# A mixture-of-experts decoder block: tile order of the late experts, and pair loads moved into the expert stage

## What is computed

```python
def _L0_ffn_ref(x, router_w, up_proj, down_proj):     # E = 8, TOP_K = 2, D = 256
    logits = jnp.einsum('nh,eh->ne', xt, router_w)
    probs = jax.nn.softmax(logits, axis=-1)
    scores, expert_idx = jax.lax.top_k(probs, TOP_K)
    scores = scores / jnp.sum(scores, axis=-1, keepdims=True)
    gate = jnp.zeros((N, E)).at[jnp.arange(N)[:, None], expert_idx].add(scores)
    h = jnp.einsum('nh,ehd->end', xt, up_proj)
    hidden = jax.nn.silu(h[..., :D]) * h[..., D:]
    out_e = jnp.einsum('end,edh->enh', hidden, down_proj)
    out = jnp.einsum('ne,enh->nh', gate, out_e)
...
x = _layernorm(x + _L0_ffn_ref(x, ...), axis=-1)
```

## Time and profile before

| | us |
| --- | --- |
| median of 3 runs | 238.61 (238.19 to 240.59) |
| profiled execution, its own time | 238.29 |
| its span, first to last instruction | 236.5 |
| PE busy | 197.6 (84%) |
| DVE busy | 162.2 (69%) |
| POOL busy | 147.9 (63%) |
| ACT busy | 116.0 (49%) |

### The profile page before, as it was taken

One profiled execution on the slowest core, in us unless ns is written; L12 is line 12 of the kernel. 1 busy time (PEld: TensorE's weight loads), 2 busy tenths in 40 slices (PEclk: granted clock), 3 DMA queues, 4 the chain that ended last, 5 costly groups with the idle time before them and its releaser, 6 DMA issues.

```text
span 236.5 us, 4774 instructions
## 1 busy us (share of the span) xinstructions
PE 197.6 (84%) x1351; PEld 175.3 (74%) x1351; DVE 162.2 (69%) x524; ACT 116.0 (49%) x296; POOL 147.9 (63%) x136
## 2 busy tenths in 40 slices
PE   7756989999999989988999999999999999970000
PEld 6646878989988878976788888888888888850000
DVE  3966688988899888674787666656656655640484
ACT  3261324525344337964887455545545544540194
POOL 0446669586596850937576477777777777541770
PEclk9999999999999999979999999999999999997555
DMA  6963356777666301213333133332332334213994
GB/s 233 394 262 136 133 206 178 240 195 241 225 182 187 85 1 62 77 14 99 92 95 109 45 93 104 113 95 75 95 111 75 92 97 107 67 35 120 413 353 181
DMA packets 18073, 33.80 MB, mean 143 GB/s; under 512 B 5662, under 2 KB 8482, under 8 KB 18050
## 3 DMA queue, kind: packets, MB, share of 16 engines
q1 hardware_dynamic: 13586, 21.80, 27.8%
q0 software_dynamic: 3744, 9.35, 13.6%
q10 hardware_dynamic: 720, 2.36, 2.6%
HBM read 25.09 MB, written 9.33 MB: 146 GB/s over the span
## 4 chain that ended last, share of the span: by engine, by line
PE 56%; DVE 12%; POOL 9%; DMA 8%; issue 7%; ACT 6%; POOLq 1%; SPq 0%; DVEq 0%; ACTq 0%
PE p_c L713 11%; PE p_y L520 6%; PE p_v L713 5%; DMA space<-y_dram 4%; POOL keep L1521 4%; POOL y_dram L1544 4%; PE p_v L463 4%; PE p_y L741 3%; PE p_s L505 3%; PE p_s L713 2%; PE p_a L713 2%; PE p_r L713 2%; PE p_c L480 2%; PE p_t L756 2%; PE p_a L536 2%
## 5 line engine op out<-in xcount | busy, mean ns | idle before, releaser
L1544 POOL DMA_INDIRECT y_dram<-keep,scatter_idx x39 | 39.1, 1002 | 20.9 <-issue 10.3
L1521 POOL DMA_INDIRECT keep<-x_dram,gather_idx x39 | 38.4, 984 | 15.5 <-issue 9.5
L713 PE MATMUL p_c<-w_hi,parts 128*128 x104 | 34.6, 414 | 0.0
L1246 DVE TENSOR_TENSOR cs<-p_c,cs 128x256 f32<-128x256 f32 x26 | 11.0, 424 | 22.3 <-ACT cs L1428 22.2
L1489 POOL TENSOR_TENSOR w_lo<-keep,w_hi 128x1536 f32 (+1 forms) x7 | 24.1, 3446 | 0.0
L1416 ACT ACTIVATE parts<-p_y 128x256 fp32r<-128x256 f32 x39 | 14.9, 381 | 18.6 <-PE p_y L741 18.6
L713 PEld LDWEIGHTS p_c<-w_hi,parts 128*128 128x128 f32 x104 | 17.6, 189 | 2.5 <-issue 0.2
L1428 ACT ACTIVATE cs<-p_c 128x256 f32<-128x256 f32 x26 | 10.0, 385 | 18.2 <-PE p_c L713 18.2
L1239 DVE TENSOR_TENSOR parts<-p_y,parts 128x256 fp32r<-128x256 f32 x39 | 16.5, 423 | 2.9 <-ACT parts L1416 2.6
L713 PE MATMUL p_v<-w_hi,parts 128*128 x52 | 17.3, 415 | 0.0
L1250 DVE TENSOR_TENSOR parts<-p_t,parts 128x256 fp32r<-128x256 f32 x39 | 16.2, 414 | 0.6 <-ACT parts L1434 0.6
(11 more groups left out here) (279 smaller groups left out, 531.2 us busy)
## 6 DMA issues: line engine op xcount, KB each, us to landing
keep<-in_weights SPq DMA_DIRECT2D x8, 768.0 KB, 4.6
space<-in_xT SPq DMA_DIRECT2D x8, 256.0 KB, 3.6
keep<-in_x SPq DMA_DIRECT2D x8, 256.0 KB, 3.3
space<-in_ctxT SPq DMA_DIRECT2D x8, 256.0 KB, 3.2
space<-in_ctxt SPq DMA_DIRECT2D x8, 256.0 KB, 3.3
x_dram<-x SPq DMA_DIRECT2D x8, 256.0 KB, 3.6
space<-y_dram SPq DMA_DIRECT2D x4, 512.0 KB, 8.0
space<-y_dram ACTq DMA_DIRECT2D x4, 512.0 KB, 8.3
```

The lines of the kernel that those rows point to most:

```text
L713: last = nc.tensor.matmul(dst, lhs[:, k, :], w[:].rearrange("p e n -> p (e n)")[:, bass.ds(start + col + k * width, width)], start=(n == 0 ...
L1521: nc.gpsimd.indirect_dma_start(xs[k % HELD], None, x2_dram, bass.IndirectOffsetOnAxis(ap=gather_idx[:, k:k + 1], axis=0)).then_inc(xs_ok[k ...
L1544: nc.gpsimd.indirect_dma_start(y_dram, bass.IndirectOffsetOnAxis(ap=scatter_idx[:, k - 2:k - 1], axis=0), xs[s][:, 0:D], None, bounds_chec ...
```

## The change

The late tiles are put in order of the group of pairs that their first row belongs to (sequences 0 to 9, 10 to 13, 14 and 15) and by expert within a group. So all rows of pairs 0 to 4 lie in the first 27 tiles and those of pairs 5 and 6 in the first 35. SP loads pair 0 when 27 tiles have been scattered, pairs 1 to 4 after one more tile each, pairs 5 and 6 after 35, and pair 7 after all 39. POOL adds pairs 0 to 4 in steps 36 to 40 of the pipeline, behind that step's scatter, and pairs 5 and 6 behind the pipeline. The sum stays in the loaded buffer, since the old place of the results still holds tiles. The late routing has more steps (a running sum over 24 counts instead of 8); `LATE_INVERSE` becomes 9, late gathers go out three tiles ahead instead of four, and POOL makes three late rows where DVE made four.

```diff
-LATE_INVERSE = 8
+LATE_INVERSE = 9
+GROUPS = 3
+FIRST_DONE, NEXT_DONE = ((b * T * TOPK + E * (P - 1)) // P for b in (EB, B - 2))
-ACT_LATE, DVE_LATE = (20, 21, 22, 23, 24, 26, 27, 28), (25, 29, 30, 31)
+ACT_LATE, POOL_LATE = (20, 21, 22, 23, 24, 26, 27, 28, 29), (25, 30, 31)
...
-            for s in range(HELD):
-                sp.wait_ge(put_ok[s], 16 * len(range(s, TILES, HELD)))
-            for j in range(0, PAIRS, 2):
+            for j in range(EB // 2):
+                wait_for_tiles(FIRST_DONE + j)
+                load_pair(j)
+            for j in range(EB // 2, PAIRS - 1):
+                wait_for_tiles(NEXT_DONE)
+                load_pair(j)
+            wait_for_tiles(TILES)
+            load_pair(PAIRS - 1)
...
                 if k == 0:
-                    running(1)
-                    note("later", nc.vector.tensor_scalar(later[:, NE:], tile_in[:, NE:], HIDE, None, ALU.add))
-                    running(2)
+                    for n in range(5):
+                        by = 2 ** n
+                        after_op("run")
+                        note("run", nc.vector.tensor_tensor(run[n + 1][:, LEAD:], run[n][:, LEAD:],
+                                                            run[n][:, LEAD - by:LEAD - by + GROUPS * E], ALU.add))
...
+            pair_scales(0, 3)
+            pair_stats(3)
+            pair_stats(4)
+            pair_moments(3)
+            pair_moments(4)
+            pair_stats(5)
+            pair_scales(3, 5)
+            pair_stats(6)
+            pair_moments(5)
+            pair_moments(6)
+            pair_scales(5, 7)
+            second_half(6)
+            dve.wait_ge(y_back[7], 16)
+            nc.vector.tensor_tensor(res[:, 7, :, :], y_all[:, 7, :, 0, :], y_all[:, 7, :, 1, :], ALU.add).then_inc(r3_ok, 1)
+            pair_stats(7)
+            pair_moments(7)
+            pair_scales(7, 8)
+            second_half(7)
...
+            pair_roots(3, 5)
+            act.wait_ge(shift3_ok, 2)
+            pair_rows(3, 2)
+            pair_rows(4, 2)
+            pair_roots(5, 7)
+            act.wait_ge(shift3_ok, 3)
+            pair_rows(5, 2)
+            pair_rows(6, 1)
+            pair_roots(7, 8)
...
-                if k + 4 == ET:
+                if k + 3 == ET:
                     pool.wait_ge(gates_saved, 64)
                     pool.wait_ge(gather_ok, 2)
-                if k + 4 >= ET and has(4):
-                    gather(k + 4)
+                if k + 3 >= ET and has(3):
+                    gather(k + 3)
...
+                if 6 <= k < 6 + len(POOL_LATE):
+                    if k == 6:
+                        pool.wait_ge(row_no_ok, 2)
+                    make_row(POOL_LATE[k - 6])
+                if k >= TILES - 3:
+                    add_pair(k - TILES + 3)
```

More of the change, by code:

```diff
@@ L220, in decoder_block @@
         full = sb("full", [P, E])
-        offset_e = sb("offset_e", [P, E])
+        need_l = sb("need_l", [P, 2, E])
+        before_ceil = sb("before_ceil", [P, E])
+        looks = sb("looks", [P, 5, E])
+        offsets = sb("offsets", [P, 2, E])
+        run = [sb(f"run{n}", [P, LEAD + GROUPS * E]) for n in range(6)]
+        wanted = turns[:].rearrange("p h d -> p (h d)")[:, 0:5 * NL * E].rearrange("p (w n e) -> p w n e", w=5, e=E)
+        found = sb("found", [P, 5, NL])
+        passed = sb("passed", [P, 2, NL])
+        moved = sb("moved", [P, 2, NL])
+        partial = [sb(f"partial{n}", [P, NL]) for n in range(2)]
+        flat = sb("flat", [P, LT])
+        wraps = [sb(f"wraps{n}", [P, LT]) for n in range(3)]
         bounds = turns[:].rearrange("p h d -> p (h d)")[:, 0:2 * NE * E].rearrange("p (w n e) -> p w n e", w=2, e=E)
         ends = sb("ends", [P, 2, NE])
-        off = back[:].rearrange("p q h d -> p (q h d)").bitcast(F16)[:, 0:(len(ACT_EARLY) + len(ACT_LATE)) * P].rearrange(
+        off = back[:].rearrange("p q h d -> p (q h d)").bitcast(F16)[:, 0:2 * len(ACT_EARLY) * P].rearrange(
             "p (n r) -> p n r", r=P)
@@ L700, in _ @@
             before(place_l[:, 0:LB, :], EB, B, False)
-            for b in range(EB, B):
-                last = above(place_l[:, b - EB + 1:, :], b, False)
+            for b in range(EB, B - 2):
+                above(place_l[:, b - EB + 1:, :], b, False)
+            above(place_l[:, LB - 1:LB, :], B - 2, False)
+            for b in range(B - 2, B):
+                last = above(place_l[:, LB + 1:, :], b, False)
             last.then_inc(place_ok, 1)
@@ L786, in _ @@
                 nc.vector.memset(upto[n][:], 0.0).then_inc(clear_ok, 1)
+            for n in range(6):
+                nc.vector.memset(run[n][:, 0:LEAD], 0.0).then_inc(clear_ok, 1)
             nc.vector.memset(eps[:], EPS).then_inc(eps_ok, 1)
@@ L1162, in _ @@
             dve.wait_ge(rank_ok, 2)
-            note("tiles", nc.vector.tensor_scalar(offset_e[:], need[:], ROUND, -ROUND, ALU.add, ALU.add))
+            note("looks", nc.vector.tensor_scalar(looks[:, 2:4, :], need_l[:], ROUND, -ROUND, ALU.add, ALU.add))
             def late_routing(k):
@@ new lines, in late_routing @@
+                if k == 2:
+                    after_op("delta")
+                    note("wanted", nc.vector.tensor_tensor(wanted, pick[:, NE:, :].unsqueeze(1).to_broadcast([P, 5, NL, E]),
+                                                           looks[:].unsqueeze(2).to_broadcast([P, 5, NL, E]), ALU.mult))
+                    gates(EB, B, 0)
+                if k == 3:
+                    after_op("wanted")
+                    note("found", nc.vector.tensor_reduce(found[:], wanted, AX_X, ALU.add))
+                    gates(EB, B, 1)
@@ L1198, in late_routing @@
                     after_op("tile_from")
-                    note("tile_no", nc.vector.tensor_tensor(tile_no[:], tile_from[:], later[:], ALU.add))
-                if k == 3 or k == 4:
-                    rows = slice(0, TOPK * B // 2) if k == 3 else slice(TOPK * B // 2, TOPK * B)
+                    note("tile_no", nc.vector.scalar_tensor_tensor(tile_no[:, 0:NE], tile_from[:, 0:NE], -HIDE, later[:, 0:NE],
+                                                                   ALU.add, ALU.add))
@@ L1202, in late_routing @@
+                if k == 6 or k == 7:
+                    rows = slice(0, TOPK * B // 2) if k == 6 else slice(TOPK * B // 2, TOPK * B)
                     after_op("tile_no")
@@ L1230, in late_routing, with pair_stats, pair_moments @@
                                             ALU.min, ALU.mult).then_inc(index_ok, 1)
+                if k == LATE_INVERSE + 3:
                     targets(inv_l, late, 1)
[L1232 removed]
+                if k == LATE_INVERSE + 4:
                     targets(inv_l, late, 2)
+                if k == TILES:
+                    pair_stats(0)
+                if k == TILES + 1:
+                    pair_stats(1)
+                    pair_moments(0)
+                    pair_stats(2)
+                    pair_moments(1)
+                    pair_moments(2)
+            def pair_stats(j):
+                dve.wait_ge(r3_ok, j + 1)
+                for q in range(2):
+                    nc.vector.bn_stats(st3[:, j, q, :], res[:, j, q, :]).then_inc(st3_ok, 1)
+            def pair_moments(j):
+                dve.wait_ge(st3_ok, 2 * j + 2)
+                for q in range(2):
+                    nc.vector.bn_aggr(mv3[:, j, q, :], st3[:, j, q, :]).then_inc(mv3_ok, 1)
             def tile(k, at, has):
@@ new lines, in _, with pair_scales @@
+            batches = [0]
+            def pair_scales(first, end):
+                js = slice(first, end)
+                batches[0] += 1
+                dve.wait_ge(sd3_ok, batches[0])
+                nc.vector.reciprocal(rs3_again[:, js, :], sd3[:, js, :]).then_inc(rs3_ok, 1)
+                nc.vector.reciprocal(rs3[:, js, :], sd3[:, js, :]).then_inc(rs3_ok, 1)
+                dve.wait_ge(rs3_ok, 2 * batches[0])
+                nc.vector.scalar_tensor_tensor(shift3[:, js, :], mv3[:, js, :, 0], -1.0, rs3_again[:, js, :],
+                                               ALU.mult, ALU.mult).then_inc(shift3_ok, 1)
@@ L1381, in distance @@
             def distance(n, place):
-                nc.scalar.activation(off[:, place, :], half[:, H_ROW:H_ROW + P], ACT.Abs, scale=-1.0,
+                nc.scalar.activation(off[:, place % (2 * len(ACT_EARLY)), :], half[:, H_ROW:H_ROW + P], ACT.Abs, scale=-1.0,
                                      bias=row_no[:, n:n + 1]).then_inc(off_ok, 1)
@@ L1548, in tile @@
                         gather(AHEAD + k - 2)
+                if 6 <= k < 6 + len(POOL_LATE):
[4 more added lines that the diff above has]
+                    add_pair(k - TILES + 3)
             tile_pipeline(tile)
-            for j in range(PAIRS - 1):
-                pool.wait_ge(y_back[j], 16)
-                nc.gpsimd.tensor_tensor(res[:, j, :, :], y_all[:, j, :, 0, :], y_all[:, j, :, 1, :], ALU.add).then_inc(r3_ok, 1)
+            for j in range(5, PAIRS - 1):
+                add_pair(j)
```

159 lines of the change are left out of this document (83 added, 76 removed).

## The result

| | before | after |
| --- | --- | --- |
| median, us | 238.43 (238.19 to 240.59) | 246.89 (244.46 to 248.76) |
| profiled execution, its own time | 238.29 | 248.76 |
| its span | 236.5 | 246.3 |
| first transposes of step 10, S(10) | 134.70 | 138.06 |
| S(30) | 185.64 | 196.22 |

The changed kernel takes 1.0295 times the time of the one before (95%: 1.0226 to 1.0364), 7.0 us more; the forecast was 241.9 us with a range of 236.8 to 246, and the measured median of 246.89 lies above both (238.29 times the ratio is 245.3, near the upper end). The profiled execution is the longest of the four and is not in this ratio, so what is read from its trace adds up to more, 9.8 us of span.

What follows compares the result with a forecast made beforehand. PE bounds the stage at 2.54 us a step, then comes a 23.3 us tail without PE work. Terms 0.9 + 8.8 + 0.5 + 3.0 - 9.6 = +3.6 on 238.29 give 241.9 us, range 236.8 to 246.

Steps and rivals of the forecast that it cites:

- Direction: Whole kernel: slower by over 1% given 0.52, within 1% 0.35, faster by over 1% 0.13.
- Gathers three ahead: Expert stage, steps 12 to 36: PE stalls for gathers issued three tiles ahead instead of four, +8.8 us, bounds 5.8 to 15.
- The closed chain: Stage: step k-1's down product decides S(k+2) through scatter and gather, so each third step pays 0.69 us, nine times.
- Routing and inverse: Step 0's extra dependent sums on DVE and the later inverse waiting for POOL's row 31: +0.9 us together.
- row 31's wait: Inverse in step 9: its last matmul needs row 31 from POOL, behind tile 6's scatter; PE waits about 0.7 us.
- Loads in the stage: Five 512 KB pair loads beside the gathers of tiles 32 to 37: +0.5 us, bounds 0 to 5.3.
- The estimate of +9: Loads in the stage by the skill page's memory latency: five gathers each up to 1.8 us more, in place of +0.5.
- Adds between the last scatters: Steps 36 to 39: POOL does a scatter and an add, 2.66 us each, and decides the pace: +3.0 us.
- The tail: From the last scatter's start to the end: 13.7 us instead of 23.3, a gain of 9.6 us.
- a clock below full between steps 1 and 40: Sign of being wrong: granted clock below full in the stage, a cost that no term of the forecast holds.
- the loads slow the gathers: Rival, steps 31 to 36: five gathers take 3.86 us instead of 2.8, +5.3 instead of +0.5, 246.7 us; chance 0.12.

## Why the prediction was right and wrong

- **Direction: right.** Slower was the likelier side, and the reason given for it, the lead, is the largest single term. With the lead alone put back, the same change is 1.2% faster than before (ratio 0.9809 to 0.995).
- **Gathers three ahead, +8.8: right.** The run without loads gives 8.9, the kernel before with a lead of three 9.7. The closed chain that was read from one free instance is there: three steps cost 0.76 us more, where 0.69 was worked out, and the mean step from S(10) to S(30) is 2.91 us, where 2.9 was said. The first clear wait is at S(13), not at S(12).
- **Routing and inverse, +0.9: right.** S(10) moved by 1.0 in the run without loads, and row 31's wait is 0.79 in the trace where 0.7 was taken. In the profile of the changed kernel itself S(10) is 3.4 later, since step 0 ran at half clock there (3.02 us for 1.65, below) and the stage itself began 0.8 later.
- **Loads in the stage, +0.5: this step failed.** It measures 2.8 us, in the steps from S(30) to S(37) at a lead of three with the clock at full. The bounds, 0 to 5.3, held it; the value was taken near the low end, on the ground that one load holds the DMA engines for only some 1.1 us. That counted what the load moves and not what becomes of a gather issued beside it. With a lead of four the median gather there lands 2.1 us later than without loads, over a stretch of seven steps; with a lead of three the gathers for which PE waits 1.82 us at S(31) and 1.70 at S(35) take 4.76 and 5.2. Why a gather is held up by so much, by a queue in the DMA engines or by the memory behind them, no run here tells.
- The Trainium skill (DMA: Bandwidth & Descriptors, Latency and other measured facts) was right in direction with its slower memory access at high load. Its figure allowed up to 1.8 us for one gather; with a lead of four the median of those beside loads rose by 2.1, from 3.6 to 5.7. The estimate of +9 from that figure was too high: 2.8 us reached PE. That the memory is what held them up is not shown.
- **Adds between the last scatters, +3.0: right, a little high.** The scatters come 2.49 apart instead of 2.66, and from S(37) to the last one it is 2.3 us more than before.
- **The tail, -9.6: right.** It is 13.4 us where 13.7 was worked out, a gain of 9.9.

With the measured terms the sum is 1.0 + 8.9 + 2.8 + 2.3 - 9.9 = +5.1 us, or +5.9 with 9.7 for the gathers, against the 7.0 of the ratio (5.4 to 8.7 by its interval). For the remaining 1.1 to 1.9 the prediction had no term. It put TensorE's clock at nothing and named a clock below full between steps 1 and 40 as a sign of being wrong. The profiled execution shows that sign in the step behind S(31); together with step 0, half clock cost it some 2.9 us (below). That the clock makes up the remainder in the other executions too was not tested. The rival "the loads slow the gathers" named the mechanism. That its 246.7 lies so near the measured median is luck, since it took 5.3 us for loads that cost 2.8 and had nothing for the clock. It had 12 chances in 100, too few for a resource of which the trace of before had no row.

## What to carry to other kernels

Where one engine issues prefetches and stores in order, the lead of a prefetch is a bound on the whole loop: follow one chain from the end of a tile to the landing of the gather it releases, and compare it with the moment of need, before giving up a tile of lead for a buffer. A load that is moved out of an idle tail into a busy stage takes its price from the transfers that have the least slack there; size it by what those transfers lose and not by the bytes alone. Look also at the pace of the engine that issues them. In the kernel before, POOL issues a gather and a scatter back to back in 2.60 us where PE's step takes 2.55, so a lead of four tiles is 4.70 us for tile 14 (137.61 to 142.31) and only 3.54 for tile 35, and the 3.86 us of the next gather then reach PE. And if the trace has no row for such an overlap, a value near one end of the bounds needs a better reason than a low share of the bandwidth.

## What was not expected of the hardware

The windows of the changed kernel, step 0, then the stalled step S(30) to S(31) with what follows, then the step up to S(32). The columns are the stretch and its length, the busy time of PE, PEld, DVE, ACT and POOL with instructions, the granted clock, the DMA engines' share and GB/s:

```profile
109.50:113.00 3.50, 3.28 (x11) 2.63 (x11) 1.39 (x10) 0.68 (x3) 2.59 (x4) 0.51 0.40 113
196.20:201.70 5.50, 3.65 (x21) 3.08 (x22) 1.77 (x5) 1.72 (x6) 3.81 (x4) 1.00 0.59 182
201.70:205.10 3.40, 3.40 (x14) 2.90 (x13) 1.19 (x3) 1.02 (x3) 1.00 (x1) 0.50 0.58 86
```

PE was busy for 3.65 of 5.5 us and had stood still for 1.82 at one go; right behind that the granted clock was 0.50 for 3.4 us, the lower of the two levels (1.2 of 2.4 GHz), and a step with no wait for a gather took 4.09 us in place of 2.54. So a late gather was paid twice, some 1.5 us more. The run with a lead of five shows it again, in its step behind the wait of 1.81:

```profile
206.10:210.04 3.94, 3.92 (x16) 3.42 (x17) 1.20 (x3) 1.42 (x4) 1.91 (x2) 0.64 0.61 232
```

It doesn't follow each such stall: behind the 1.70 at S(35) of the changed kernel the clock stays at 1.00 and the step takes 2.99, and with POOL's rows earlier the same steps wait 1.59 and 1.48 us at 1.00. In step 0 of the changed kernel the clock fell as well, and that step took 3.02 us in place of 1.65; in the profiled execution with a lead of four steps 0 and 1 took 3.02 and 3.22 us (1.65 and 2.27 before) at 0.50 and 0.53. What sets it off in one execution and not in another stays open.
